# Local attention of a Macaron block: two looped stages against one written-out pipeline

## The reference

```
logits = einsum('bld,kd->blk', x, W) + b        # K = 32 offsets
w = softmax(logits, axis=-1)
xp = pad(x, ((0, 0), (0, K - 1), (0, 0)))
out = sum over d of w[:, :, d:d + 1] * xp[:, d:d + L]
```

## Time and profile before

| | us |
|---|---|
| median of 3 runs | 2650.3 |
| the profiled execution itself | 2660.06 |
| its span | 2658.3 |
| PE busy in the span | 2112.5 (79%) |
| DVE busy | 1864.1 (70%) |
| ACT busy | 882.9 (33%) |
| POOL busy | 879.2 (33%) |
| granted PE clock, mean | 0.862 |

### The profile page before, as it was taken

One profiled execution on the slowest core, in us unless ns is written; L12 is line 12 of the kernel. 1 busy time (PEld: TensorE's weight loads), 2 busy tenths in 40 slices (PEclk: granted clock), 3 DMA queues, 4 the chain that ended last, 5 costly groups with the idle time before them and its releaser, 6 DMA issues. The chain is left out here.

```text
span 2658.3 us, 42460 instructions
## 1 busy us (share of the span) xinstructions
PE 2112.5 (79%) x11491; PEld 1370.8 (52%) x11492; DVE 1864.1 (70%) x3770; ACT 882.9 (33%) x1720; POOL 879.2 (33%) x880
## 2 busy tenths in 40 slices
PE   2699986668999865888868578989889875688885
PEld 1466655335666554666746323333333365466664
DVE  5799966027889676666887577767677457666696
ACT  1222212002222222333326435555555522233332
POOL 1344431004444355555524500000000025655541
PEclk6799995558999956999989779989899985799998
DMA  4000000200000151222324733334333015122234
GB/s 155 1 0 0 0 1 0 38 10 0 0 0 0 39 182 43 79 79 77 111 89 101 148 45 58 51 61 61 53 50 50 2 44 180 46 79 79 77 117 141
DMA packets 110145, 156.07 MB, mean 59 GB/s; under 512 B 20646, under 2 KB 77260, under 8 KB 109516
## 3 DMA queue, kind: packets, MB, share of 16 engines
q1 hardware_dynamic: 90304, 104.43, 17.7%
q0 software_dynamic: 17472, 48.80, 5.7%
q10 hardware_dynamic: 2252, 1.29, 0.2%
HBM read 107.00 MB, written 47.20 MB: 58 GB/s over the span
## 5 line engine op out<-in xcount | busy, mean ns | idle before, releaser
L1833 DVE TENSOR_REDUCE t_nm<-ps 128x1 f32<-128x512 f32 (+3 forms) x768 | 390.7, 552 | 144.7 <-PE ps L1923 87.4
L1899 ACT ACTIVATE t_E<-ps 128x1024 f32<-128x1024 f32 (+3 forms) x384 | 295.3, 808 | 269.9 <-PE ps L1949 215.9
L1328 PE MATMUL ps<-m_w,m_xT 128*128 (+1 forms) x1248 | 350.7, 417 | 1.1 <-issue 1.1
L1328 PEld LDWEIGHTS ps<-m_w,m_xT 128*128 128x128 f32 x1248 | 224.9, 191 | 56.4 <-issue 4.5
L535 PE MATMUL ps<-wgT,f_xT 128*128 128x352 f32 x512 | 181.0, 500 | 37.8 <-DVE f_h L437 35.7
L1946 PE MATMUL ps<-t_Qs,t_Ks 98*128 98x512 bf16 (+3 forms) x768 | 205.7, 349 | 5.4 <-DMA t_Qs<-t_mT 3.6
L496 POOL TENSOR_TENSOR f_h<-f_h,f_hmagic 128x704 f32<-128x704 f32 x64 | 108.0, 1688 | 290.1 <-DVE f_h L182 290.1
L1348 PE MATMUL ps<-m_w,m_hT 128*128 (+1 forms) x1248 | 202.2, 298 | 1.3 <-DVE m_hT L1427 1.3
L569 PE MATMUL ps<-wdT,f_hT 128*128 128x256 f32 (+1 forms) x768 | 191.4, 391 | 7.4 <-DVE X L472 5.4
L1818 POOL COPY t_Va<-t_V 128x128 f32 (+1 forms) x64 | 16.1, 295 | 533.8 <-DVE t_mp L1844 533.3
L1415 DVE TENSOR_TENSOR m_ab<-ps,m_b 128x512 f32<-128x512 f32 x208 | 143.2, 689 | 66.8 <-issue 55.8
(11 more groups left out here) (279 smaller groups left out, 4157.2 us busy)
## 6 DMA issues: line engine op xcount, KB each, us to landing
m_yl<-m_picked_out SPq DMA_DIRECT2D x64, 256.0 KB, 2.9
m_raw<-in_L_ffn_rw SPq DMA_DIRECT2D x48, 256.0 KB, 3.4
t_parts<-t_qkv_part SPq DMA_DIRECT2D x64, 192.0 KB, 2.8
t_Qs<-t_parts SPq DMA_DIRECT2D x96, 128.0 KB, 4.1
t_Ks<-t_parts SPq DMA_DIRECT2D x96, 128.0 KB, 6.2
m_rows<-m_xn SPq DMA_DIRECT2D x16, 512.0 KB, 4.3
m_xg<-m_rows POOLq DMA_DIRECT2D x64, 128.0 KB
X<-in_L_attn_x SPq DMA_DIRECT2D x4, 1024.0 KB, 14.2
```

Of the source, the lines that this page charges most:

```text
L1328: last = nc.tensor.matmul(ps[:, H1 + u, :], xT[:, u, kx, k, :], of_expert(w1, kw, e, k), start=n == 0, stop=n == 3 * DC - 1)
L1833: nc.vector.tensor_reduce(dst, ps[:, bank, 0:n], AX_X, ALU.max, negate=True).then_inc(emptied, 1)
L1899: nc.scalar.activation(E[:, s % NPB, :, 0:n], ps[:, bank:bank + 2, 0:n], ACT.Exp, scale=float(HD) ** -0.5).then_inc(e_ok, 1)
```

## The change

The two blocks become one, without hardware loops: all 8 groups are written out, in 12 rounds (k = 0 to 11), in which each engine works on several groups at once. All addresses are constants. `XN` has one normalisation, by ACT (Identity with scale and shift), and both the logits and the output read it; `xn` is gone. POOL also makes the shift. `Wn` goes to DRAM a group at a time, and each group's band is read back after its own write has landed. `spillT` has 128 rows, of which rows 32 to 127 are cleared once by POOL, and the spill's product takes all 128 rows of the next tile. Banks: 0 and 1 turned x, 2 logits, 3 turned band, 4 turned spill, 5 and 6 output, each once and not twice. Logits, small sums, statistics and bands have two buffers.

The core of the diff (declarations and the removed lines, which the listing above shows, are left out):

```diff
             def _(dve):
...
+                for k in range(GROUPS + 4):
+                    if on(k):
+                        shift_logits(k)
+                    if on(k + 2):
+                        x_stats(k + 2)
+                    if on(k):
+                        weights(k)
+                    if on(k - 3):
+                        add(k - 3)
...
+                def x_scale(g):
+                    b = g % 2
+                    pool.wait_ge(stats, g + 1)
+                    if g >= 2:
+                        pool.wait_ge(xn_ok, g - 1)
+                    nc.gpsimd.tensor_tensor(rstd[:, b, :], veps[:, b, :], ch.minus_half[:, :], ALU.pow)
+                    nc.gpsimd.drain()
+                    nc.gpsimd.tensor_tensor(shift[:, b, :], nmean[:, b, :], rstd[:, b, :], ALU.mult
+                                            ).then_inc(rstd_ok, 1)
+                x_scale(0)
+                nc.gpsimd.memset(spillT[:, :, :], 0.0).then_inc(cleared, 1)
                 ch.clear(pool, "fp4_")
+                for g in range(1, GROUPS):
+                    x_scale(g)
...
+                def band_turn(g):
+                    u = g % 2
+                    pe.wait_ge(band_in[u], 16 * (g // 2 + 1))
+                    if g:
+                        pe.wait_ge(b_stored, g)
...
+                def out(g):
+                    u = g % 2
+                    pe.wait_ge(b_stored, g + 1)
+                    if g + 1 < GROUPS:
+                        pe.wait_ge(xn_ok, g + 2)
+                    if g:
+                        pe.wait_ge(added, g)
+                    for j in range(GT):
+                        n = g * GT + j
+                        o = ps[:, OUT + j // 2, (j % 2) * D:(j % 2 + 1) * D]
+                        spill = n % TPB < TPB - 1
+                        last = nc.tensor.matmul(o, bandT[:, u, j * P:(j + 1) * P], XN[:, n, :], start=True, stop=not spill)
+                        if spill:
+                            last = nc.tensor.matmul(o, spillT[:, u, j * P:(j + 1) * P], XN[:, n + 1, :],
+                                                    start=False, stop=True)
+                    last.then_inc(out_ok, 1)
+                x_turn(0)
+                logits(0)
+                for k in range(GROUPS + 4):
+                    if on(k - 2):
+                        band_turn(k - 2)
+                    if on(k + 1):
+                        x_turn(k + 1)
+                    if on(k - 3):
+                        out(k - 3)
+                    if on(k + 1):
+                        logits(k + 1)
...
+                def x_normalise(g):
+                    b = g % 2
+                    act.wait_ge(rstd_ok, g + 1)
+                    for j in range(GT):
+                        last = nc.scalar.activation(XN[:, g * GT + j, :], ch.tile(g * GT + j), ACT.Identity,
+                                                    bias=shift[:, b, j:j + 1], scale=rstd[:, b, j:j + 1])
+                    last.then_inc(xn_ok, 1)
...
+                x_normalise(0)
+                x_store(0)
+                act.wait_ge(cleared, 1)
+                for k in range(GROUPS + 4):
+                    if on(k + 1):
+                        x_normalise(k + 1)
+                    if on(k):
+                        exp(k)
+                    if on(k - 2):
+                        band_store(k - 2)
+                    if on(k + 1):
+                        x_store(k + 1)
...
+                for g in range(GROUPS):
+                    tiles = slice(g * GT, (g + 1) * GT)
+                    sp.wait_ge(w_ok, g + 1)
+                    sp.dma_start(rows[:, tiles, 0:WIN], Wn[:, tiles, :]).then_inc(banded, 16)
+                    if g >= 2:
+                        sp.wait_ge(b_turned, g - 1)
+                    sp.wait_ge(banded, 16 * (g + 1))
+                    sp.dma_start(band[:, g % 2, :, :], bands[:, tiles, :]).then_inc(band_in[g % 2], 16)
```

More of the change, by code:

```diff
@@ L653, in local_attention, with on @@
             sem, ("stats", "rstd", "xn", "x_turned", "x_stored", "logits", "shifted", "exp", "weights"))
-        banded = sem("banded")
+        banded, b_turned, b_stored, out_ok, added, cleared = map(
+            sem, ("banded", "b_turned", "b_stored", "out", "added", "spill_cleared"))
+        band_in = [sem("band_in0"), sem("band_in1")]
         with nc.Block() as block:
[L656 to L659, removed]
+            def on(g):
+                return 0 <= g < GROUPS
@@ new lines, in weights, with add @@
+                def weights(g):
+                    b = g % 2
+                    dve.wait_ge(exp_ok, g + 1)
+                    reduce(small[:, b, 1, :], lg[:, b, :, :], AX_X, ALU.add)
+                    drain()
+                    nc.vector.reciprocal(small[:, b, 2, :], small[:, b, 1, :])
+                    drain()
+                    tt(Wn[:, g * GT:(g + 1) * GT, :], lg[:, b, :, :], over_window(g, 2), ALU.mult).then_inc(w_ok, 1)
+                def add(g):
+                    dve.wait_ge(out_ok, g + 1)
+                    for k in range(2):
+                        xs = ch.X[:, g * GT + 2 * k:g * GT + 2 * k + 2, :]
+                        last = tt(xs, xs, ps[:, OUT + k, :].rearrange("p (j d) -> p j d", j=2), ALU.add)
+                    last.then_inc(added, 1)
@@ L704, in _, with x_turn @@
+                x_scale(0)
+                nc.gpsimd.memset(spillT[:, :, :], 0.0).then_inc(cleared, 1)
                 ch.clear(pool, "fp4_")
[L706 to L709, removed]
+                for g in range(1, GROUPS):
+                    x_scale(g)
             @block.tensor
             def _(pe):
-                def step(g, end):
+                def x_turn(g):
@@ L739, in _, with exp, band_store @@
-                turns(act, step)
+                def exp(g):
+                    act.wait_ge(shifted, g + 1)
+                    nc.scalar.activation(lg[:, g % 2, :, :], lg[:, g % 2, :, :], ACT.Exp).then_inc(exp_ok, 1)
+                def band_store(g):
+                    u = g % 2
+                    act.wait_ge(b_turned, g + 1)
+                    if g >= 2:
+                        act.wait_ge(out_ok, g - 1)
+                    nc.scalar.activation(bandT[:, u, :], ps[:, BAND, :], ACT.Copy)
+                    nc.scalar.activation(spillT[0:WIN, u, :], ps[0:WIN, SPILL, :], ACT.Copy).then_inc(b_stored, 1)
@@ L744, in _ @@
                 rows = ch.skewed.rearrange("(n p c) -> p n c", n=TILES, p=P)
[L745 to L752, removed]
```

156 lines of the change are left out of this document (55 added, 101 removed).

## The result

| | before | changed |
|---|---|---|
| median, us | 2653.32 (2646.83 to 2663.92, 4 runs) | 2564.27 (2558.12 to 2568.85, 4 runs) |
| ratio to before | | 0.9649, 95% interval 0.9623 to 0.9676 |
| profiled execution, us | 2660.06 | 2565.47 |
| its span, us | 2658.3 | 2563.6 |
| granted PE clock, mean | 0.862 | 0.89 |

The forecast was 2556 (2543 to 2592), and 2566 for the profiled execution. The total fits to 0.3%. Its parts fit less well.

The account below looks back on a forecast made before the run. Before: waits set the first block, DMA alone took 17.7 us, half-clock PE filled the second; afterwards PE would bound full-clock rounds of 7.5 us. Rounds summed to a stage of 92, not 186: 2650.3 - 94 = 2556 us (2543 to 2592).

Parts of the forecast that it names:

- The filling and rounds 0 to 2: Start of the changed stage, 396.2 to 431.3 us: a chain at half clock, then rounds of 6.75, 6.75 and 8.5.
- Round 3: Round with the first output group: 11.9 us, its products 5.5 at half clock and the rest at full, to 443.2.
- the clock rises during the first output group: PE's clock in round 3: expected to go from half to full during the first output products and stay up.
- Rounds 4 to 6: Full-clock rounds of 7.5 us, 0.45 less where a group ends a batch: 21.4, plus 0.9 for handovers, to 465.5.
- Rounds 7 to 10 and the last add: Rounds without x, 17.2 us including about 1 waiting for the last band, then 1.4 for the last add, to 484.1.
- The 4 us for a falling clock: Allowance added to the stage for stretches in which the clock falls back, taking its end from 484.1 to 488.
- The split of the gain by cause: Of 94 us: 17.7 exposed write, about 35 clock, some 18 faster product issue, the rest overlap of the blocks.
- The faster issue of the products for some 18: Output products: constant addresses and 128 rows take an instruction at half clock from 0.575 to 0.43 us; some 18 us gained.
- Rival (a): Clock stays at half in the changed stage: 63 us gained, 2587, or 46, 2605, with the old 0.575; chance 0.2.
- Rival (b): On ACT, Identity and the exponential share no table: two loads a round, some 3 us in all, 2559; chance 0.04.
- Rival (c): DRAM round trip doesn't shrink and becomes the bound: 17 us gained, 2633, or slower, 2667; chance 0.02 each side of 19.9.
- The whole change is what this stage becomes: Claim that the edited stage, closed off by meeting points at both ends, alone changes: 92 us and not 186.

Follow-up runs that it names:

- e1: The kernel before with only the spill's product widened to 128 rows (spillT cleared once), both looped blocks kept; 2613.69 us (one run).
- e3: The changed kernel with the spill's product reading 32 rows again; 2585.68 us (4 runs), ratio to before 0.9708.
- e6: The changed kernel with output and add handed over bank by bank; 2564.07 us (one run).
- e4: The kernel before with each group's weights written to DRAM as soon as ready, only the end of the first block waiting for them; 2644.63 us (one run).
- e2: The kernel before with the second block written out, so product addresses are constants, the spill keeping 32 rows; 2649.17 us (one run).
- e10: e5 run once more, unedited, beside e9; 2531.32 us (5 runs), ratio to before 0.954.
- e9: The changed kernel run once more, unedited, beside e10; 2572.82 us (5 runs), ratio to before 0.9681.
- e11: The changed kernel with VectorE normalising, bank-by-bank output and add, and extra transposes keeping TensorE at work in the filling; 2550.54 us (5 runs), ratio 0.9597.
- e8: The changed kernel with output and add handed over bank by bank and extra transposes keeping TensorE at work in the filling; 2547.03 us (5 runs), ratio 0.9558.
- e5: The changed kernel with the normalisation back on VectorE instead of ScalarE; 2541.35 us (4 runs), ratio to before 0.9543.

## Why the prediction was right, and where it was not

**The filling and rounds 0 to 2**: forecast 35.1 us, measured 34.2, at half clock but for the first 3.4 us, before PE's first instruction: as priced.

**Round 3**: forecast 11.9, measured 8.5. The step that failed is "the clock rises during the first output group". It was up before that group began. PE had worked without a gap from 432.14, first logits, then transposes, and the first product pair ran at full speed at 438.86. In the rounds before, a wait of 1.17 us for ScalarE's copy lay in each. What I took from the earlier trace rows as the condition for the rise, the 128-row products at their quicker pace, is enough for it in the old loop (e1) and not needed for it here: the clock was up before any output product, in this kernel and in e3, which has 32 rows in the spill.

**Rounds 4 to 6**: forecast 22.3 with handovers, measured 20.0. The allowance of 0.9 for handovers was not needed, as PE never waits. The rest is 6.9 us for a full round and not 7.5: turning band and x costs 0.90 and 0.88, sixteen products 3.45, and the logits 1.71 when the next work follows at once.

**Rounds 7 to 10 and the last add**: forecast 18.6, measured 20.6. I counted 1 us for the last band and nothing for PE waiting on the add. The add is 1.28 us and was hidden by turning and logits; when these run out it stands in the open, 2.65 us in three waits. e6 took all three away, which confirms them; part of that gain went to a wait of 1.08 us for a band.

**The 4 us for a falling clock**: none, it is 1.00 from round 4 to the end. The forecast's 92 for the stage was thus 9 us too long, of which 0.9 is the filling, 3.4 round 3, 2.3 rounds 4 to 6 and 4 the allowance, against 2.0 lost in the tail.

**The split of the gain by cause** was partly wrong. The write: 17.7 forecast with its read; e4 takes 11.2 of it and keeps 6.45 in the open (its stage is 13.2 shorter, with the 2 us of the clock). "The faster issue of the products for some 18", put down to constant addresses together with the rows: e2 shows that constant addresses give at most 0.8 us. The rest is the rows, by the 0.3 us a pair at half clock and 0.2 at full. The clock and the rows together are 45 us in the old loop (e1), against 53 in my split. If their gains add up, e1 and e4 leave some 44 us to the overlap of the blocks; that part was not measured by itself.

**Rival (a)**, half clock throughout, stood at 0.2. e3 shows how near it was: with 32 rows the clock falls back twice. The Trainium skill's rule (TensorE: Matmul & The Clock Gate, What's actually happening) is that the gate follows how busy PE has been. If busy is what the profile shows, the rule does not account for e1, where PE is busy 7.21 of 8.50 us before the clock rises, against 10.00 of 10.00 in the earlier trace rows without a rise. But the profile counts 1.15 us as busy for a pair that takes 0.85 on full rows, so it can't tell whether PE worked through all of it. The prediction was too quick to say that the trace contradicts the rule. Whether the rows or the slower pace kept the clock down was not separated by any run. That few rows alone don't keep it down is shown by e10: from 1660 to 1680 us PE mixes products on 48, 98 and 128 rows, in bf16, at 1.00. **Rival (b)** did not come: there is one table load, of 1.28 us, at 412.29, under a wait. **Rival (c)** neither: the writes take 2.6 us, and PE never waits for a band.

In the slices of the profile before, the digits of VectorE for the local attention (slices 6 to 8) are 6, 0 and 2, where the text ahead of the prediction has 9, 6 and 0; no number was worked out from them.

**The total** was right to 8 us in the median, and that closeness is luck, through two errors that cancel: the stage gained 103 and not 94, and the causal attention lost 10.6, though I had held that the edited stage, closed off by meeting points, could change nothing outside. "The whole change is what this stage becomes" was the step that failed. It also means that this kernel leaves up to 40 us in a stage that nobody edited (e10 against e9: 41.5 us in the medians, 44.8 in the causal attention).

## What to carry to other kernels

A product on few rows between products on all rows can cost more than a full one, twice over: by the change itself, and, as in the loop before, by a clock that stays low; pad with zeros where the operand is free, and try this first, because it is a small edit (45 of 103 us here). In a written-out pipeline look at the last rounds by themselves: waits that the main work hides come into the open there. And when a small edit moves a stage that it doesn't touch, look for waits on "issue" that return with each turn of a loop, and compare the packet counts of the instruction queues, before believing any account of the edit itself: here the stage with such stops was 45 us longer than without (e9 and e10).

## What the runs showed of the hardware that was not expected

- Changing between 128 and 32 rows: a pair of f32 instructions of 256 columns every 1.15 us and not 0.85 at half clock, every 0.63 and not 0.43 at full clock, with constant addresses or with loop registers.
- The granted clock stayed 0.50 for 95.7 us of a loop on such mixed rows, with stretches of PE busy 10.00 of 10 us, and was 1.00 with PE busy 29.10 of 37.60 on full ones. In e3 it also stood at 1.00 for some 40 us of mixed rows.
- VectorE stopped 2.6 to 3.5 us twice a loop turn in one kernel, up to 9.6 in another with ten more instructions ahead of the loop, and not at all in a third; TensorE likewise 3.1 to 3.9 us once a turn in the kernel before. What would place the code well was not tried. Why e11's causal attention is 618 us and e8's 608, with the same kind of stop, stays open; two executions of one kernel differ by nearly as much (593 and 584, e5 and e10).
- The fastest program of the study is e5 (e10), 2531 us, whose causal attention is the only one without these stops. The shortest local attention is e11's, 73.7 us.
